# Attention's second part starts with chunks that are still on chip; the input is loaded first and step 0 prepared beside the convolution

## The reference

```python
x = x + conv_ssm_0(gn(x))     # in_proj 96->2*192, 3x3 depthwise conv, SiLU, 4-direction selective scan,
x = x + conv_ssm_1(gn(x))     # LayerNorm, gate by silu(z), out_proj 192->96; 2nd: other scan orders
t = t + attn_2(ln(t)); t = t + ffn_2(ln(t))     # linear attention, 6 heads; FFN in fp8/fp16 steps
t = t + attn_3(ln(t)); t = t + ffn_3(ln(t))
# selective scan, over L = 4096 pixels, for 4 directions k, 192 channels d, 16 states n:
h = exp(dt * A) * h + (dt * u) * B
y = sum_n(h * C) + D * u
# attention without softmax: y = q @ (k^T v) * 16**-0.5, so all tokens' k^T v is summed first
```

## Time and profile before

| | |
|---|---|
| median of 3 runs | 11526.75 us (11501.28 to 11531.94) |
| the profiled execution | 11522.77 us, span 11520.9 us |
| busy | PE 77%, DVE 88%, ACT 61%, POOL 85% |
| mean granted clock of TensorE | 0.74 of full speed |
| DMA | 1631.73 MB, mean 142 GB/s |

### The profile page before, as it was taken

The page is one execution under the profiler, slowest core; times in us unless marked ns, Lnnn a source line. Parts: engine busy times, 40 slices in busy tenths (PEclk is TensorE's granted clock), DMA queues, the critical chain, the costliest instruction groups (busy, mean ns, idle before and its releaser), DMA issues.

```text
span 11520.9 us, 94504 instructions
## 1 busy us (share of the span) xinstructions
PE 8853.6 (77%) x26272; PEld 2221.2 (19%) x26272; DVE 10175.8 (88%) x6086; ACT 6996.5 (61%) x10714; POOL 9737.9 (85%) x4231
## 2 busy tenths in 40 slices
PE   6876677876888667869777787788788877777757
PEld 2211111211112111212112121122111221122213
DVE  3899998999889998989999899899988999898873
ACT  4665555665556555667556765566755666567654
POOL 3899988899888998989988888888888888998860
PEclk8875577875778667769677796788677876777766
DMA  3666688666775565655776668956687565665550
GB/s 100 143 136 135 140 154 153 150 136 142 159 154 147 131 159 148 157 131 142 171 157 146 133 149 151 161 146 141 137 162 150 140 151 138 160 159 120 123 137 14
DMA packets 1781801, 1631.73 MB, mean 142 GB/s; under 512 B 1323982, under 2 KB 1325296, under 8 KB 1781276
## 3 DMA queue, kind: packets, MB, share of 16 engines
q1 hardware_dynamic: 1781276, 1625.69, 63.9%
HBM read 625.58 MB, written 194.51 MB: 71 GB/s over the span
## 4 chain that ended last, share of the span: by engine, by line
PE 22%; DVE 21%; issue 20%; POOL 20%; ACT 8%; SPq 4%; DMA 3%; DVEq 0%; POOLq 0%; ACTq 0%
POOL pr L1645 14%; DVE hs L1566 9%; DVE ps L1551 7%; DVE hs L1562 4%; PE ps L1032 4%; PE ps L861 3%; PE ps L826 3%; PE ps L1019 3%; PE ps L1010 2%; POOL bup L1659 2%; PE ps L994 2%; POOL dur L1659 2%; POOL us L1636 2%; ACT dec L1289 2%; SPq L720 1%
## 5 line engine op out<-in xcount | busy, mean ns | idle before, releaser
L1645 POOL TENSOR_TENSOR pr<-hs,crep 128x1024 f32<-128x1024 f32 x3072 | 7184.8, 2355 | 1202.5 <-PE ps L1032 587.2
L1566 DVE TENSOR_TENSOR_SCAN hs<-dec,carry,ps 128x1024 f32<-128x1024 f32 x1728 | 4054.2, 2346 | 232.6 <-POOL pr L1645 7.0
L1551 DVE TENSOR_TENSOR ps<-ps,dur 128x1024 f32<-128x1024 f32 x2304 | 2789.4, 1211 | 524.1 <-PE ps L1019 384.0
L1019 PE MATMUL ps<-sbc,selb 96*128 96x512 bf16 x4608 | 1842.0, 492 | 1788.5 <-DVE hs L1566 1240.2
L1289 ACT ACTIVATE dec<-dtr,ac 128x1024 f32<-128x1024 f32 x2304 | 2610.7, 1136 | 436.5 <-DVE hs L1566 424.4
L1032 PE MATMUL ps<-pr,red 128*32 128x512 f32 x12288 | 2288.3, 828 | 25.4 <-POOL pr L1645 20.1
L1296 ACT ACTIVATE carry<-hs 128x1 f32<-128x1 f32 x2304 | 457.0, 199 | 2422.7 <-DVE hs L1566 2249.5
L1566 DVE TENSOR_TENSOR_SCAN hs<-dec,zero,ps 128x1024 f32<-128x1024 f32 x576 | 1351.3, 2346 | 84.7 <-ACT dec L1289 14.6
L826 PE MATMUL ps<-xb,tapw 96*96 96x512 f32 x2304 | 1184.8, 636 | 54.4 <-ACT sd L1122 51.9
L1019 PEld LDWEIGHTS ps<-sbc,selb 96*128 96x128 bf16 x4608 | 381.6, 108 | 3922.4 <-DVE hs L1566 2304.2
L1289 ACT ACTIVATE ps<-dtr,ac 128x1024 f32<-128x1024 f32 x768 | 848.3, 1105 | 399.3 <-DVE hs L1566 399.3
(11 more groups left out here) (227 smaller groups left out, 7621.3 us busy)
## 6 DMA issues: line engine op xcount, KB each, us to landing
dtr<-de SPq DMA_DIRECT2D x768, 512.0 KB, 7.9
dur<-us SPq DMA_DIRECT2D x768, 512.0 KB, 8.6
crep<-bc_d SPq DMA_DIRECT2D x512, 512.0 KB, 6.6
ust<-u_d SPq DMA_DIRECT2D x256, 384.0 KB, 6.0
y_d<-yst SPq DMA_DIRECT2D x768, 128.0 KB, 3.5
sd<-y_d SPq DMA_DIRECT2D x448, 192.0 KB, 5.2
brep<-bc_d SPq DMA_DIRECT2D x128, 512.0 KB, 5.8
u_d<-sd SPq DMA_DIRECT2D x64, 384.0 KB, 3.2
```

The source lines that it names most:

```text
L1019: mm = pe.matmul(ps[:, SLOT + 2 * (n % RS) + hf, :], selb[:, i % GT // 2, :], sbc[:, w % 2, B * hf:B * (hf + 1)], start=True, stop=True)
L1551: dve.tensor_tensor(slot(n), slot(n), dur[:, 2 * (G % 2) + i % 2, :], ALU.mult).then_inc(bu_v, 1)
L1566: dve.tensor_tensor_scan(hs[:, n % RH, :], dec[:, others(n) % RD, :], slot(n), init, ALU.mult, ALU.add).then_inc(scan_v, 1)
L1645: pool.tensor_tensor(pr[:, n % RP, :], hs[:, n % RH, :], crep[:, q, :], ALU.mult).then_inc(prod_g, 1)
```

## The change

Three things. (1) Start: five loads (semaphore `first_in`) go first, then the image, then the other 45. The wait for `w_in` and the preparing of constants move behind the group norm on ACT and DVE, and to tick `FIRST` = 28 on PE. (2) Step 0: `prepare(0)` goes; its parts are issued at ticks 28 to 42 of the head, so its first half stands between the last chunk's convolution matmuls; `load_u(0)` follows the store of chunk 1, `load_u(1)` the last tick of the head. (3) Attention beside a scan: part 2 takes the chunks in the order 6, 7, 0, 1, ..., 5. 6 and 7 are still in `tnl[0]` and `tnl[1]`, and are neither stored nor loaded; the others go round four buffers (two new ones over the norm's scratch in `sd`), two of the loads are issued ahead of the middle and four in ticks 3 to 6 of part 2. The copies and the second matmul of the middle are each a tick or two later, the middle's length is the same.

```diff
+    if w == 0:
+        return FIRST + 2, FIRST + 4, 1, FIRST + 9, FIRST + 14
+    return (8, 11, 2, 21, 33) if late(w) else (-10, -6, 4, 14, 33)
...
+FIRST = PRE_GN + 2 * MM // HEAD_RATE + 2
+FIRST_TICKS = FIRST + 15
...
-        tnl = [sd[0:CH + 1, 2048 + B * r:2048 + B * (r + 1)] for r in range(2)]
+        tnl = [sd[0:CH + 1, at:at + B] for at in (2048, 2048 + B, 0, B)]
...
+        def a2_chunk(p, overlapped):
+            return (p + C8 - 2) % C8 if overlapped else p
...
# SP, attn
-                        if overlapped and tick - a1_every(overlapped) * c == 6:
+                        if overlapped and c < C8 - 2 and tick - a1_every(overlapped) * c == 6:
...
+                def t_load(p):
+                    c = a2_chunk(p, True)
+                    sp.dma_start(tnl[p % 4][0:CH, :], t_d[b, l][:, B * c:B * (c + 1)]).then_inc(t_in[p % 4], 16)
                 if overlapped:
                     for r in range(2):
-                        sp.wait_ge(t_out[r], 16 * (N + 1) * C8 // 2)
+                        sp.wait_ge(t_out[r], 16 * (N + 1) * (C8 // 2 - 1))
+                    sp.wait_ge(at_v, M + C8)
+                    t_load(2)
+                    t_load(3)
+                for _ in range(4):
+                    yield
                 for tick in range(A2_TICKS):
-                    if overlapped and tick < C8:
-                        after(sp, ao_p, M + tick - 1)
-                        sp.wait_ge(kv_p, 2 * (M + C8))
-                        sp.dma_start(tnl[tick % 2][0:CH, :], t_d[b, l][:, B * tick:B * (tick + 1)]).then_inc(t_in[tick % 2], 16)
+                    if overlapped and 3 <= tick < 7:
+                        sp.wait_ge(ao_p, M + tick - 2)
+                        t_load(tick + 1)
                     yield
...
# SP, start
             head = beside(plan[0], stages, False)
-            for _ in range(HEAD_TICKS):
+            load_first()
+            next(head)
+            load_rest()
+            for tick in range(1, HEAD_TICKS):
                 next(head)
-            load_u(0)
+                if tick == FIRST:
+                    load_u(0)
+            load_u(1)
             store_c(0, 0)
...
             load_b(0)
-            load_u(1)
...
# PE, start
-            for _ in range(HEAD_TICKS):
-                next(head)
-            prepare(0)
+            for tick in range(FIRST_TICKS):
+                if tick == FIRST:
+                    pe.wait_ge(w_in, NWEIGHTS * 16)
+                    pe.wait_ge(set_v, SET_V)
+                if tick < HEAD_TICKS:
+                    next(head)
+                prepare_at(tick, 0)
             fill(0)
...
# PE, attn, part 2
-                        if overlapped:
-                            pe.wait_ge(t_in[c % 2], 16 * (m // 2 + 1))
-                        after(pe, ao_v, m - 1)
+                        if overlapped and p >= 2:
+                            pe.wait_ge(*t_landed(p, N))
+                        after(pe, ao_v, M + p - 1)
...
# ACT, start
-            for _ in range(HEAD_TICKS):
-                next(head)
-            prepare(0)
+            for tick in range(FIRST_TICKS):
+                if tick == PRE_GN:
+                    act.wait_ge(first_in, NFIRST * 16)
+                    act.wait_ge(w_in, NWEIGHTS * 16)
+                    act.activation(ac[:, :, :, :], ac[:, :, :, :], ACT.Exp).then_inc(set_a, 1)
+                if tick == FIRST:
+                    act.wait_ge(set_v, SET_V)
+                if tick < HEAD_TICKS:
+                    next(head)
+                prepare_at(tick, 0)
...
# DVE, middle of attn
                 yield
+                yield
                 dve.wait_ge(mid_p, 2 * N + 1)
                 dve.tensor_copy(mm_, ps[0:CH, SB, 0:CH]).then_inc(mid_v, 1)
                 yield
+                yield
                 dve.wait_ge(mid_p, 2 * N + 2)
                 dve.tensor_copy(pp, ps[0:CH + 1, SB + 1, 0:CH]).then_inc(mid_v, 1)
-                yield
-                yield
```

More of the change, by code:

```diff
@@ L520, in _, with load @@
             n = 0
-            def load(dst, src):
+            def load(dst, src, landed=w_in):
                 nonlocal n
-                sp.dma_start(dst, src).then_inc(w_in, 16)
+                sp.dma_start(dst, src).then_inc(landed, 16)
                 n += 1
[L527 to L549, removed]
@@ L785, in _ @@
         def _(pe):
-            pe.wait_ge(w_in, NWEIGHTS * 16)
-            pe.wait_ge(set_v, SET_V)
+            pe.wait_ge(first_in, NFIRST * 16)
             def side_banks(done):
@@ L1037, in prepare_at @@
                 if w < W:
-                    _, first, apart, second = prep_places(w)
+                    _, first, apart, second, _ = prep_places(w)
                     for hf, at in ((0, first), (1, second)):
@@ L1087, in _ @@
         def _(act):
-            act.wait_ge(w_in, NWEIGHTS * 16)
             act.preload_act_table_set("natural_log_exp_and_others")
-            act.activation(ac[:, :, :, :], ac[:, :, :, :], ACT.Exp).then_inc(set_a, 1)
-            act.wait_ge(set_v, SET_V)
+            act.wait_ge(set_g, SET_G)
             def pre(j, overlapped):
@@ L1308, in prepare_at @@
                 if w < W:
-                    gathers, first, apart, second = prep_places(w)
-                    late = apart // 2
+                    gathers, first, apart, second, sizes = prep_places(w)
+                    late = max(1, apart // 2)
                     if place in (gathers, gathers + 1):
@@ L1321, in prepare_at @@
                                 keep_z(h, hf, w)
-                    if place == 33:
+                    if place == sizes:
                         softplus(w)
[L1325 to L1334, removed]
-            head = beside(plan[0], stages, False)
-            for _ in range(HEAD_TICKS):
-                next(head)
-            prepare(0)
+            head = beside(plan[0], stages, False)
+            for tick in range(FIRST_TICKS):
[8 more added lines that the diff above has]
+                prepare_at(tick, 0)
             for place in range(-10, 0):
@@ L1372, in _ @@
         def _(dve):
[L1373 to L1395, removed]
             def pre(j, overlapped):
@@ L1567, in states @@
                                            ALU.mult, ALU.add).then_inc(scan_v, 1)
+            dve.wait_ge(first_in, NFIRST * 16)
+            dve.tensor_tensor(tap, tap, wx[:, 0, :].unsqueeze(1).to_broadcast([CH, TAPS, D]), ALU.mult)
             head = beside(plan[0], stages, False)
-            for _ in range(HEAD_TICKS):
+            for _ in range(PRE_GN):
+                next(head)
+            dve.wait_ge(w_in, NWEIGHTS * 16)
+            dve.tensor_copy(selb[:, :, :], selb_f)
+            dve.tensor_copy(neg[:, :, :], neg_f)
+            dve.tensor_copy(w1q[:, :, :], w1_f, saturate=False)
+            dve.tensor_copy(w2q[:, :, :, :], w2_f, saturate=False)
+            dve.tensor_copy(b1_8, b1_f, saturate=False)
+            dve.tensor_copy(b2_8, b2_f, saturate=False)
+            dve.tensor_tensor(dsum[:, :, :], ds_k[:, :, 0, :], ds_k[:, :, 1, :], ALU.add).then_inc(set_v, 1)
+            for k in range(2, K):
+                dve.wait_ge(set_v, k - 1)
+                dve.tensor_tensor(dsum[:, :, :], dsum[:, :, :], ds_k[:, :, k, :], ALU.add).then_inc(set_v, 1)
+            dve.tensor_copy(b1q[:, :, :], b1_8)
+            dve.tensor_copy(b2q[:, :], b2_8)
+            dve.wait_ge(set_v, K - 1)
+            for l in range(2):
+                for h in range(2):
+                    dve.tensor_scalar(dg[:, l, h, :], eye[:, :], dsum[:, l, h:h + 1], None, ALU.mult)
+            dve.wait_ge(set_a, 1)
+            dve.tensor_scalar(ac[:, :, :, :], ac[:, :, :, :], -1.0, None, ALU.mult).then_inc(set_v, 1)
+            dve.wait_ge(set_v, SET_V - 1)
+            dve.wait_ge(set_g, SET_G)
+            dve.memset(sd[CH:CH + 1, 2048:3072], 1.0)
+            dve.memset(sd[CH:CH + 1, 0:1024], 1.0).then_inc(set_v, 1)
+            for _ in range(PRE_GN, HEAD_TICKS):
                 next(head)
```

87 lines of the change are left out of this document (57 added, 30 removed).

## The result

The changed kernel took 11428.28 us (median of 5 runs, 11420.33 to 11453.93), the kernel before 11526.75 (5 runs beside it, 11501.28 to 11538.35): ratio 0.9924, 95% interval 0.9909 to 0.9938. The prediction was 11441, range 11405 to 11486. In two further comparisons, 5 runs each, the same changed kernel was at 0.9932 (0.9919 to 0.9945) and 0.9938 (0.9925 to 0.9950), with medians 73 and 69 us under the kernel before. So the 98 us of the first comparison are the high end. Pooled, the 27 executions before and the 15 changed ones have medians of 11519.71 and 11442.17: the change is worth some 78 us.

What follows compares the result with a forecast made beforehand. DVE was taken to set the pace in the loop, while time saved before the first recurrence comes off whole. 11522.77 less 47.7 us (start: 19.1 + 16.7 + 11.9) and 34 us (attention) gave 11441, range 11405 to 11486.

Steps and rivals of the forecast that it cites:

- (a): Start: with the input's load issued ahead of 45 others, the input lands at 18.5 us, 19.1 us earlier.
- Rival 2: Start: the input shares the engines with the weights and lands at 29, saving 8.5 us; total 11452; chance 0.1.
- (b): Start: step 0's first half prepared beside the convolution brings softplus 16.7 us earlier, 95.9 us after the convolution's start.
- from the start of that `x_dbl` to softplus it took 12.9: Start: the second half's `x_dbl` to softplus, 12.9 us before the change, was taken to stay, putting softplus at 95.9.
- Rival 3: Start: the mix with the convolution costs as much as it hides, saving 0 to 5 us; total 11455; chance 0.08.
- (c): Start: step 1's load is there in time, so softplus to first recurrence takes 18.4 instead of 30.25 us, 11.9 less.
- Attention: Six loop steps with part 2: DVE's waits at the additions fall from 45.0 to about 10 us, saving 34.
- the 10.2 and 11.3 us go: Part 2 in N = 0 and 4: the last load moves ahead of SP's tile 18, so these waits vanish.
- Rival 1: Part 2: the wait moves to loads landing behind `dur` and `crep` transfers; attention gives 12 us, total 11463; chance 0.2.
- The sum: Whole kernel: 47.7 us from the start and 34 from attention, taking 11522.77 to 11441.
- Rival 4: End of attention's part 1: SP's new wait for chunk 7 holds the next step's loads; slower, 11561; chance 0.02.
- Rival 5: One part doesn't take place, for instance PE at tick 28 waits for late constants; total 11489; chance 0.05.

Runs made afterwards that it cites:

- input_last: Changed kernel with the input's transfer issued behind all 50 loads again: first recurrence at 165.3 us, 11479.35 us in one execution.
- store_first: Changed kernel with `store_c(0, 0)` issued ahead of `load_u(1)` instead of behind it: first recurrence at 140.6 us, 11434.26 us in one execution.
- u1_last: Changed kernel with `load_u(1)` put back behind `load_b(0)`: first recurrence at 153.0 us, 11462.70 us in one execution.
- attn_only: Kernel before with only the attention part of the change, the start as before: 32 us below the kernel before, ratio 0.9973.
- loads_earlier: Changed kernel with part 2's four late loads issued one tick earlier, at ticks 2 to 5: 82 us below the kernel before, ratio 0.9925.
- two_buffers: Changed kernel with chunk order 6, 7, 0 to 5 kept but only two buffers: 11458.74 us, ratio 0.9951 to the kernel before.

## Why the prediction was right

**(a) The input first.** Forecast 19.1 us, measured 20.0 (46.90 to 26.94), and input_last takes 19.3 of it away again. The reason held: the transfers behind it on the same queue didn't take its share. In the trace all DMA packets that start between 6.0 and 15.5 us are the input's (384 of 4096 B, the last ending at 16.7), and those of the next load, 96 of 2048 B, start at 15.6. The rate while it lands, in a view of the stretch from its issue on (length, PE busy, clock, DMA share, GB/s):

```profile
4.50:14.00 9.50, 0.00 (x0) 1.00 0.94 150
```

Rival 2, the shared engines with a landing at 29, is out by that and by the landing at 17.6. The Trainium skill (DMA: Bandwidth & Descriptors, "Anatomy of one DMA") gives its formula under a heading on DMAs that GpSimd issues, which my prediction left out; by it this load, issued by SP, would have landed at about 12, an estimate, and the trace's 13.1 us from issue to landing speaks against it again. What I had wrong is the weights: "their data some us later" than 28 was 37.3, and the point from which I said ACT would be late was 38. It was nearer, at some 37.5: ACT has first to use them itself (37.36 to 37.72), and its eviction could start at 37.92. That cost nothing by 0.2 us, which is luck.

**(b) The first half beside the convolution.** Forecast 16.7, measured 12.3: softplus at 127.19 is t = 100.25 and not 95.9. The mix itself went as worked out: the convolution ends at t = 76.0 (forecast 77), the second half's `x_dbl` starts at 82.9 (forecast 83), though PE's gap ahead of it was 3.2 us and not some 5. The step that failed is the sentence "from the start of that `x_dbl` to softplus it took 12.9". It took 17.3, for the wait of 4.4 us on `store_c(0, 0)`, which stands behind `load_u(1)`. I had costed that move of a load by what it frees and looked for what it is moved past only on the far side (`load_group`, `load_b`). On the near side was the store, whose landing ACT waits for. store_first takes that back: 4.8 to 5.3 us. Rival 3, that the mix costs what it hides, is out: PE's part of it was 2.9 us.

**(c) Step 1's load in time.** Forecast 11.9, measured 30.25 - 18.73 = 11.5, and DVE's own multiplication, with `dur` just landed, is what comes last, as said; u1_last brings the wait of 11.75 us for ACT back.

**Attention.** Forecast 34 us, of waits 45.0 to 10; measured 45.0 to 22.9, and 23.6 us in the lengths of the six steps. N = 1 (4.5 forecast to stay, 5.3 stayed) and N = 5 (5.6, 7.2) were near. The term that was mis-sized is that of N = 0 and 4, "the 10.2 and 11.3 us go": 2.7 and 3.2 stayed, and their steps came to 94.2 and 95.1, not 90. I had taken the whole sum for the last load. It was 8.3 and 8.0 us of it; the remainder, 1.9 and 3.3 us, was waits for PE itself at the first two additions, and those are still there (1.5 and 1.2 in N = 0, 1.5 and 1.7 in N = 4). The 90 was also below my own terms: 102.1 - 10.2 and 103.0 - 11.3 are 91.9 and 91.7. N = 3 went the other way: it had no waits before and 4.2 us in this profile, 1.5 in the next two. PE waited for no load there; its granted clock was lower (below). Rival 1, that the wait moves to the loads behind `dur`, is true of N = 5 and in part of N = 1 (PE waited 6.9 us for chunks there) and of no other.

**The sum** was 82: 48 and 34. The parts measure 44 (by the first recurrence) and 24 (by the steps), which is 68, and 40 and 32 by the medians of the kernels with one part. The total of three comparisons is 98, 73 and 69. My two misses are both on the side of too much, 4 us at the start and 10 in attention. Of the first two profiles they are made up by the 18.7 us that no part accounts for. So the mechanism was right in its main terms, but that 11428 and 11441 lie so near is luck: the later comparisons put the change at 73 and 69 us, below the 82.

Rival 4, SP held at its new wait, shows in one layer and costs nothing there. In N = 0 SP issued the first of the early loads 0.1 us after its stores to `y_d`, without waiting. In N = 1 it stood 6.2 us at the new wait, in attn_only and in each of the three executions of the changed kernel (6.1 in one). SP's waits in the changed kernel from 6220 to 6245 (what SP waited for: us in total, times, longest):

```profile
SPq L747 <- ACT de L1303: 10.2, 1, 10.2
SPq L690 <- DVE sd L1496: 6.2, 1, 6.2
```

L690 is the wait for chunk 7; the early loads go out at 6230.69, and SP's next issue, for the next step at 6241.69, waited 10.2 us more for ACT. So the forecast that SP comes to that wait behind DVE was wrong for N = 1, and its cost of 0 right. Rival 5 is out too: the constants were ready at 42.6, PE came to tick 28 some 40 us later.

## What to carry to other kernels

When one DMA issue is moved forward in a queue, list what it now stands ahead of, and for each of these who waits for its landing: a load with a late condition of its own holds a store that was ready. A wait that is the sum of several should be split by instruction before it is forecast to go, because only the part with the named cause goes. And where a queue's program order blocks behind another engine's pace, one tick in the place of an issue can be worth 5 us (N = 5 in loads_earlier), and together with two loads issued earlier 8 us (N = 0 and 4 in two_buffers against the changed kernel).

## What the hardware showed that I had not expected

**An issue right behind a large transfer can block for long.** The issue behind the input's took 8.66 us (5.26 to 13.92) against 0.4 for its neighbours, and 8.1 to 8.7 us in the eleven profiles of kernels that load the input first. For that long SP could do nothing else. The weights were 8 us later for it, and it ended well before the input had landed (17.6). The input is 1.57 MB and its destination rows are 64 floats; whether the size, the short rows or both are the reason no run here tests.

**The waits of part 2 move with TensorE's granted clock.** The same 16 matmul records (line 952 before, 988 after) in N = 3, before and in the changed kernel: stretch, length, PE busy, granted clock, DMA share and rate.

```profile
9435.00:9460.00 25.00, 9.82 (x16) 0.77 0.42 97
```

```profile
9370.00:9395.00 25.00, 12.52 (x16) 0.62 0.35 73
```

At 0.77 they took 9.82 us, at 0.62 12.52, in a stretch in which PE has gaps of 1 to 2 us waiting for DVE ahead of them; DVE's waits there were 0 and 4.2 us. In the changed kernel the clock stood at the lower of its two levels (1.2 GHz, 0.5 in the trace) from 9358.2 to 9388.9. Over the 14 profiles, from N = 3's first matmul to its last, a mean clock of 0.86 to 0.89 goes with no waits, 0.80 to 0.81 with 0.5 to 1.5 us and 0.58 with the 4.2; kernels with the same attention stand in more than one of these groups. This is read from the traces; no run sets the clock.

**Unchanged code differs by 10 to 50 us between executions.** The steps without part 2 took 10324 to 10376 us over the 14 profiles, one of each kernel or repeat, the end behind the last recurrence 378 to 389. For a change of this size the profile's own clocks (first recurrence, waits by line) are the better measure: the first recurrence of the changed kernel came at 145.9, 145.4 and 145.4.
